# Three decay buffers and four state buffers in the scan loop of a decoder layer

## The chip, the cores and the metric

The kernel runs on one core of one Trainium2 chip. The metric is the device time of one execution in microseconds (us). A profile is one more execution of the same program, and all durations below come from it.

The engines are called as in the profile: PE (TensorE, matrix products and transposes into PSUM; PEld is its weight load), DVE (VectorE), ACT (ScalarE), POOL (GpSimd) and SP (SyncE, which here issues every DMA). Each engine runs its own instructions strictly in order and waits on semaphores that the others raise.

## The reference, cut to what matters

Eight sequences of 512 tokens with 256 channels go through one layer: a Mamba block, a slot attention with a GRU (three rounds), and a feed-forward block with a spiking output, each with a layer norm behind it. The part that the change touches is the selective scan of the Mamba block:

```
dt = softplus(dt_in @ W_dt.T + dt_bias)          # 512 tokens x 512 channels
dA  = exp(dt[..., None] * A)                     # "decay", 16 states for each channel
dBu = dt[..., None] * Bm[:, :, None, :] * u[..., None]
def step(h, e):
    da, dbu, c = e
    h = da * h + dbu                             # recurrence over the 512 tokens
    y = jnp.einsum('bdn,bn->bd', h, c)
    return h, y
```

Everything is float32.

## The kernel before, in words

The core works through the sequences one after the other, and the three blocks are software-pipelined: the body for step i runs the Mamba block of sequence i, the slot attention of sequence i-1, the first part of the feed-forward block of sequence i-2 and its spiking output (one step later, so of i-3). Steps 0 to 2 fill the pipeline (step 0 has the Mamba block alone, step 1 adds the attention, step 2 the feed-forward block), steps 3 to 7 hold all of it, and steps 8 to 10 have no Mamba block. At the end of each step all engines meet (`meet`).

The channels lie in 4 chunks of 128 (c), and the 16 states of a chunk in 8 pairs, so there are 32 groups g in a step, g = 8c + q. A group is one tile of 128 partitions x 1024 (two states x 512 tokens). The body walks through 35 slots, and each engine runs its part of slot g and then the "filler" of that slot: pieces of the other two blocks, which a table called `plan` places by hand at slot numbers. Per group the engines do this:

- ACT, line 875, `decay(g)`: two exponentials of 128x511 into the decay buffer `d_a[g % 2]`. In slot g it makes the decay of group g + 1 and then runs its filler. Its wait is `scan_done >= g - 1` for decay(g), which in slot g means that the scans 0 to g - 1 are done.
- DVE, line 1069, `mul(g)`: B x dt x u into PSUM (pb banks 1 and 2). It waits for the B rows (`bb`, three buffers, DMA) and for scan g - 1.
- DVE, line 1078, `scan(g)`: the recurrence, reads `d_a` and pb, writes `h[g % HR]`. It waits for the decay (`da_ready`), and from g = HR on for `hsum_done >= g - HR + 1`: PE must have read the buffer.
- POOL, line 443: h x C in place, raises `hc_done`.
- PE, line 645, `hsum(g)`, placed LAG = 2 slots later: eight transposes of 128x128 that add the states in PSUM bank py, raises `hsum_done`.

In slot g DVE runs scan(g), mul(g + 1) and then its filler. Behind each chunk ACT copies py to `yv` (line 888), PE transposes it back into pc (`y_back`, line 655), DVE adds u x D (line 1095, "ypost") and POOL multiplies by the gate (line 447). The feed-forward products of slot 10 and later (line 623 "up", line 631 "down") wait for ypost, because they share bank pc.

Fillers that the prediction's steps touch, with their slots:

- `gate_x` of the attention rounds 0, 1, 2 in slots 2/4, 13/15, 24/26: PE line 554, then tanh on ACT line 778 (a table load in front of it), and on ACT also lines 782 to 786 (`reset`, `keep`). `sp_ln` in slot 2 (ACT line 808) makes the softplus of the chunks 1 to 3, and POOL line 425 (`dt`) adds it up in slots 3, 6, 6.
- `keep` on POOL (line 405) in slots 4, 15, 26; `hold` on DVE (line 994) and `cand_x` on PE (line 564) in slots 6, 17, 28; `cand` in slots 7, 18, 29: tanh on ACT (line 812), then POOL lines 409 and 412, which finish the new slots state hT (`h_done`).
- `sq` and `norm` (ACT line 764, PE lines 527 and 528, ACT 769 and 771) start the next round behind `h_done`, in slots 9 and 20; `score` on DVE (line 975) in slots 10 and 21, `soft` (line 981) one slot later, `colsum`, `recol`, `spread`, `renorm` (PE 534, DVE 984 and 986, PE 539, DVE 989) in the two or three slots behind it.
- `out_stats` in slot 4 (DVE lines 916 to 921, then POOL line 393) and `out_norm` in slot 8 (DVE line 927, four tensor_scalars of 128x256 on tile reg_m), in steps 3 to 7 only.
- Weight merging on PE and ACT in slot 10 of step 0 only.

`reg_a` is one SBUF region for several uses: the first 2060 columns are the padded input `upad` of the convolution before the scan, and the decay buffers lie on the same columns. `xp` is a copy of the projected dt, B and C rows; it is read by the dt projection and by the DMAs to DRAM before the first group.

Of the kernel before, what the change touches and what calls it, by code (L numbers as in the profile page):

```python
# [26 lines left out]
ACT = mybir.ActivationFunctionType  # L27
AX = mybir.AxisListType

P = 128  # L30
BATCH, L, E = 8, 512, 256
DIN, NS, DTR, KC = 512, 16, 16, 4
# [6 lines left out]
GROUPS = DT * PAIRS  # L39
# [1 line left out]
SCALE = float(E) ** -0.5  # L41
LN_EPS, RMS_EPS = 1e-5, 1e-6
BETA, THRESHOLD, STEPS = 0.9, 1.0, 5
HR = 3
HB = 3
Q = 32

# [48 lines left out]
def decoder_layer(nc, bc_dram, x, ctx_in, cols_d, w_inT, w_xT, w_dtT, w_outT, wq_d, wk_d, wv_d, wihT, whhT, w_fcT, w_prT, out):  # L96
    with ExitStack() as ctx:
        def sb(name, shape, dt=F32):
            return ctx.enter_context(nc.sbuf_tensor(name, shape, dt))

        def ps(name, shape):
            return ctx.enter_context(nc.psum_tensor(name, shape, F32))
# [12 lines left out]
        neg_a = sb("neg_a", [P, DT * NS])  # L115
# [6 lines left out]
        rms_eps = sb("rms_eps", [P, 1])  # L122


        reg_a = sb("reg_a", [P, 2060 + HR * 1024])
        reg_y = sb("reg_y", [P, DT, L])
        upad = reg_a[:, 0:2060].rearrange("p (c t) -> p c t", c=DT)
        d_a = reg_a[:, 0:2048].rearrange("p (s n t) -> p s n t", s=2, n=2)
        h = reg_a[:, 2060:].rearrange("p (s n t) -> p s n t", s=HR, n=2)
        h2 = reg_a[:, 2060:].rearrange("p (s t) -> p s t", s=HR)  # L130
        d_a2 = reg_a[:, 0:2048].rearrange("p (s t) -> p s t", s=2)
        xn = reg_y[:, 0:2, :].rearrange("p a (b e) -> p (a b) e", e=E)
        xnT = reg_y[:, 2:4, :]
        sp = reg_y
# [5 lines left out]
        dt = sb("dt", [P, DT, L])  # L140
        dtu = sb("dtu", [P, DT, L])
        cb = sb("cb", [P, NS, L])
        xp = sb("xp", [P, L])
        bb = sb("bb", [P, HB, 2, L])
        x1 = sb("x1", [P, TT, E])
        hT = sb("hT", [P, ET, L])
# [25 lines left out]
        pb = ps("pb", [P, 4, L])  # L172
# [11 lines left out]
        s = {n: ctx.enter_context(nc.semaphore(n)) for n in COUNTS}  # L184
# [12 lines left out]
        def col(name, j):  # L197
            return cols[:, COLS[name].start + j:COLS[name].start + j + 1]
# [46 lines left out]
        def chunk_end(g):  # L245

            c, r = divmod(g - LAG, PAIRS)
            return c - 1 if 1 <= c <= DT and r == 0 else None
# [61 lines left out]
        def take(position, slot_step, mamba, slots, ffn, spikes):  # L310

            for step in plan.get(position, ()):
                kind = step[0]
                if (spikes if kind in SPIKE_STEPS else ffn if kind in FFN_STEPS else mamba if kind in MAMBA_STEPS else slots):
                    if kind in ("up", "down"):
                        slot_step(*step, back=chunks_back(position) if mamba else 0, spikes=spikes, mamba=mamba)
                    else:
                        slot_step(*step, spikes=spikes, ffn=ffn, mamba=mamba)
# [63 lines left out]
        def _(pool):  # L382
# [44 lines left out]
            def body(i, mamba, slots, ffn, spikes):  # L427
# [10 lines left out]
                for g in range(SLOTS):  # L438
                    if mamba and g < GROUPS:
                        q = g % PAIRS  # L440
                        pool.wait_ge(s["scan_done"], g + 1)
                        pool.wait_ge(s[f"cb_in{q}"], 16)
                        pool.tensor_tensor(h[:, g % HR], h[:, g % HR], cb[:, 2 * q:2 * q + 2], ALU.mult).then_inc(s["hc_done"], 1)  # L443
                    if mamba and chunk_end(g) is not None:
# [14 lines left out]
        def _(pe):  # L459
# [175 lines left out]
            def hsum(g):  # L635
# [6 lines left out]
                for j in range(2):  # L642
                    for i2 in range(TT):
                        cols_ = slice(i2 * P, (i2 + 1) * P)
                        mm = pe.matmul(py[:, cols_], h[:, g % HR, j, cols_], ident[:], is_transpose=True,  # L645
                                       start=(q == 0 and j == 0 and i2 == 0), stop=(q == PAIRS - 1 and j == 1), skip_group_check=True)
# [66 lines left out]
        def _(act):  # L713
# [105 lines left out]
            def body(i, mamba, slots, ffn, spikes):  # L819
                def filler(position):  # L820
                    take(position, slot_step, mamba, slots, ffn, spikes)

                filler("start")
                def u_tanh(j):
                    act.wait_ge(s["conv_step"], 6 * (j // 2) + 5 + j % 2)
                    act.activation(dtu[:, j], u2[:, j], ACT.Tanh, scale=0.5).then_inc(s["uth_ready"], 1)

                def z_tanh(j):
                    act.wait_ge(s["z_full"], j + 1)
                    act.activation(sz[:, j], z_banks[j], ACT.Tanh, scale=0.5).then_inc(s["zth_ready"], 1)  # L830

                def softplus_parts(c):
                    act.wait_ge(s["pre_full"], 2 + c)
                    act.activation(dt[:, c], pb[:, c, :], ACT.Relu, bias=col("dt_bias", c))
                    act.activation(sp[:, c], pb[:, c, :], ACT.Abs, bias=col("dt_bias", c)).then_inc(s["sp_abs"], 1)  # L835

                if mamba:
                    z_tanh(0)
                    z_tanh(1)
                    z_tanh(2)  # L840
                    u_tanh(0)
                    u_tanh(1)
                    z_tanh(3)
                filler("z")
                if mamba:
                    u_tanh(2)
                    u_tanh(3)
                filler("u")
                if mamba or slots:
                    act.preload_act_table_set(LN_EXP)  # L850
                if mamba:
                    act.wait_ge(s["pre_full"], 1)
                    act.activation(xp[:], pb[:, 2, :], ACT.Copy).then_inc(s["bc_kept"], 1)
                filler("x")
                if mamba:

                    softplus_parts(0)
                    act.wait_ge(s["sp_abs"], 1)
                    act.activation(sp[:, 0], sp[:, 0], ACT.Exp, scale=-1.0).then_inc(s["sp_exp"], 1)
                    act.wait_ge(s["sp_exp"], 1)  # L860
                    act.activation(sp[:, 0], sp[:, 0], ACT.Ln, bias=1.0).then_inc(s["sp_ln"], 1)  # L861
                    for c in range(1, DT):
                        softplus_parts(c)
                filler("dt")

                def decay(g):
                    c, n = g // PAIRS, 2 * (g % PAIRS)
                    if g == 0:
                        act.wait_ge(s["da_zero"], 1)
                    if g % PAIRS == 0:  # L870
                        act.wait_ge(s["dt_ready"], c + 1)
                    if g >= 2:
                        act.wait_ge(s["scan_done"], g - 1)
                    for j in range(2):
                        ins = act.activation(d_a[:, g % 2, j, 1:], dt[:, c, 1:], ACT.Exp, scale=neg_a[:, c * NS + n + j:c * NS + n + j + 1])  # L875
                    ins.then_inc(s["da_ready"], 1)

                for g in range(SLOTS):
                    if mamba:
                        if g == 0:  # L880
                            decay(0)
                        if g + 1 < GROUPS:
                            decay(g + 1)
                        if g > LAG and (g - LAG) % PAIRS == PAIRS - 1:
                            c = (g - LAG) // PAIRS
                            act.wait_ge(s["hsum_done"], PAIRS * (c + 1))
                            act.wait_ge(s["dt_ready"], DT)
                            act.activation(yv[:, c], py[:], ACT.Copy).then_inc(s["yt_ready"], 1)
                        if g == MERGE_SLOT and not slots:
                            merge_weights()  # L890
                    filler(g)
                filler("end")
                if mamba:
                    next_copies()
                    act.wait_ge(s["upad_zero"], 1)
                    u_copies(0)
                    u_copies(1)
                    if slots:
                        act.wait_ge(s["x_full"], 4 + XR * NI + 1)
                    for e in range(ET):  # L900
                        act.wait_ge(s["post_full"], e + 1)
                        act.activation(hT[:, e], px[:, e, :], ACT.Copy).then_inc(s["hT_loaded"], 1)
                    u_copies(2)
                    u_copies(3)
                meet(act, i + 2)

            iterations(act, body)


        @block.vector  # L910
        def _(dve):
# [114 lines left out]
            def body(i, mamba, slots, ffn, spikes):  # L1026
# [45 lines left out]
                def scan(g):  # L1072

                    dve.wait_ge(s["da_ready"], g + 1)
                    dve.wait_ge(s["mul_done"], g + 1)
                    if g >= HR:
                        dve.wait_ge(s["hsum_done"], g - HR + 1)
                    dve.tensor_tensor_scan(h2[:, g % HR], d_a2[:, g % 2], pb[:, 1:3, :].rearrange("p a t -> p (a t)"), 0.0,  # L1078
                                           ALU.mult, ALU.add).then_inc(s["scan_done"], 1)

                for g in range(SLOTS):
                    if mamba:
# [9 lines left out]
                        if chunk_end(g) is not None:  # L1092
                            c = chunk_end(g)
# [59 lines left out]
```

## Time and profile before

| | |
|---|---|
| median of 3 runs | 1865.69 us (1863.43 to 1866.33) |
| the profiled execution, its own time | 1863.23 us |
| its span, first to last instruction | 1861.2 us |
| busy: PE, DVE, ACT, POOL | 1366.2, 1350.9, 987.5, 898.0 us |
| DVE line 1078 (scan), 256 times | 584.6 us, 2283 ns each |
| DVE line 1069 (mul), 256 times | 314.6 us, 1229 ns each |
| POOL line 443, 256 times | 611.7 us, 2391 ns each |
| ACT line 875, 512 times | 335.6 us |
| mean granted clock of PE | 0.849 |

Busy time is a sum over the whole span. No engine is busy all the time: the shares of the two fullest are 73%. So the waits between them, read in order of time, say more than the sums.

### The profile page before, as it was taken

The page shows a single profiled execution, that of the slowest core. Times are in us where ns is not written, and L with a number is a line of the kernel's source. Part 1 is how long each engine was busy: PE and PEld are TensorE (multiplying, and loading weights), DVE is VectorE, ACT ScalarE, POOL GpSimd, SP SyncE. Part 2 cuts the span into 40 slices and gives each one's busy share as a digit, 9 for nine tenths or more (in the row PEclk, how much of TensorE's full clock was granted, in tenths as well). Part 3 has the DMA queues.
Part 4 walks back from the last instruction along what each step waited for, and adds up shares of the span by engine and source line. Part 5 has one row for each costly group of instructions (what it writes and reads, how often), then busy time and mean ns, then how long its engine had stood idle before and what let it go on. Part 6 is the DMA issues. An engine that isn't in the chain of part 4 may idle for free.

```text
span 1861.2 us, 16320 instructions
## 1 busy us (share of the span) xinstructions
PE 1366.2 (73%) x5472; PEld 826.3 (44%) x5472; DVE 1350.9 (73%) x1509; ACT 987.5 (53%) x1519; POOL 898.0 (48%) x459
## 2 busy tenths in 40 slices
PE   5555767686797758885778667887588857786975
PEld 2344344453455335552456334553355434562433
DVE  3987588957876888867888687867878778773142
ACT  4432665547663655647554655637465566534532
POOL 0665077615764266624666165642667155651110
PEclk9555978897899879998799978998799978998988
DMA  5632343205330532206321343305332153310000
GB/s 182 241 124 79 100 163 118 86 26 214 113 109 27 189 108 102 80 24 204 113 101 56 120 136 114 106 23 183 102 112 79 36 193 112 112 34 0 12 0 23
DMA packets 64762, 188.89 MB, mean 101 GB/s; under 512 B 6224, under 2 KB 22480, under 8 KB 64720
## 3 DMA queue, kind: packets, MB, share of 16 engines
q1 hardware_dynamic: 64720, 188.37, 29.3%
q8 instruction: 22, 0.36, 0.1%
q14 instruction: 20, 0.16, 0.0%
HBM read 183.62 MB, written 4.72 MB: 101 GB/s over the span
## 4 chain that ended last, share of the span: by engine, by line
PE 40%; DVE 31%; ACT 15%; issue 6%; POOL 5%; DMA 2%; ACTq 0%; DVEq 0%; POOLq 0%; SPq 0%; another core or an unknown queue 0%
DVE reg_a L1078 16%; DVE pb L1069 8%; PE py L645 6%; PE pc L631 5%; PE pc L623 4%; PE pb L486 4%; PE pb L605 3%; POOL reg_a L443 3%; ACT reg_a L875 2%; PE px L549 2%; PE px L527 2%; DMA x_out<-reg_m 2%; PE pb L587 2%; ACT xs L778 2%; DVE reg_m L927 1%
## 5 line engine op out<-in xcount | busy, mean ns | idle before, releaser
L443 POOL TENSOR_TENSOR reg_a<-reg_a,cb 128x1024 f32<-128x1024 f32 x256 | 611.7, 2391 | 438.1 <-DVE reg_a L1078 437.8
L1078 DVE TENSOR_TENSOR_SCAN reg_a<-reg_a,pb 128x1024 f32<-128x1024 f32 x256 | 584.6, 2283 | 143.5 <-ACT reg_a L875 110.2
L875 ACT ACTIVATE reg_a<-dt,neg_a 128x511 f32<-128x511 f32 x512 | 335.6, 711 | 165.3 <-DVE reg_a L1078 164.6
L645 PE MATMUL py<-ident,reg_a 128*128 128x128 f32 x2048 | 329.9, 318 | 70.6 <-POOL reg_a L443 70.6
L645 PEld LDWEIGHTS py<-ident,reg_a 128*128 128x128 f32 x2048 | 288.9, 167 | 167.6 <-POOL reg_a L443 104.9
L1069 DVE TENSOR_TENSOR pb<-bb,pb 128x1024 f32<-128x1024 f32 x256 | 314.6, 1229 | 29.7 <-ACT reg_y L835 2.6
L564 PE MATMUL pb<-ex,vw 64*128 64x512 f32 x48 | 46.9, 1075 | 146.9 <-DVE px L994 146.9
L623 PE MATMUL pc<-x2T,w_fc 128*128 128x512 f32 x224 | 119.0, 658 | 28.1 <-DVE reg_y L1095 21.2
L549 PE MATMUL px<-hT,whh 128*128 128x512 f32 x288 | 137.4, 613 | 0.4 <-ACT xs L778 0.4
L631 PE MATMUL pc<-w_pr,reg_m 128*128 128x256 f32 x448 | 109.8, 396 | 7.0 <-ACT y_sb L798 4.1
L405 POOL TENSOR_TENSOR xs<-xs,hT 128x1024 f32<-128x1024 f32 x24 | 56.6, 2358 | 96.2 <-ACT xs L786 96.2
L527 PE MATMUL px<-hT,gT 128*64 128x512 f32 x96 | 61.1, 772 | 56.8 <-ACT xs L764 56.8
L631 PEld LDWEIGHTS pc<-w_pr,reg_m 128*128 128x128 f32 x448 | 86.1, 200 | 24.6 <-ACT y_sb L798 6.5
L793 ACT ACTIVATE reg_m<-pc 128x512 f32<-128x512 f32 x56 | 33.3, 595 | 115.1 <-PE pc L623 103.0
L425 POOL TENSOR_TENSOR dt<-dt,reg_y 128x512 f32<-128x512 f32 x32 | 40.7, 1283 | 102.7 <-ACT reg_y L861 95.8
L549 PEld LDWEIGHTS px<-hT,whh 128*128 128x128 f32 x288 | 55.2, 200 | 70.6 <-issue 66.2
L778 ACT ACTIVATE xs<-px,half_b 128x512 f32<-128x512 f32 x72 | 46.7, 681 | 63.8 <-PE pb L554 46.3
L564 PEld LDWEIGHTS pb<-ex,vw 64*128 64x128 f32 x48 | 11.3, 293 | 154.4 <-DVE px L994 154.4
L549 PE MATMUL pb<-hT,whh 128*128 128x512 f32 x96 | 56.4, 719 | 31.8 <-ACT reg_y L835 31.8
L486 PE MATMUL pb<-reg_y,w_in 128*128 128x512 f32 x144 | 67.3, 612 | 11.1 <-ACT reg_y L728 11.1
L1042 DVE SCALAR_TENSOR_TENSOR u<-reg_a,cols,u 128x512 f32<-128x512 f32 x96 | 64.2, 740 | 11.2 <-SPq L332 11.2
L623 PEld LDWEIGHTS pc<-x2T,w_fc 128*128 128x128 f32 x224 | 41.8, 207 | 64.2 <-issue 35.1
(174 smaller groups left out, 2259.5 us busy)
## 6 DMA issues: line engine op xcount, KB each, us to landing
bb<-bc_rows SPq DMA_DIRECT2D x256, 512.0 KB, 3.7
cb<-bc_rows SPq DMA_DIRECT2D x64, 512.0 KB, 6.0
xin<-x_in SPq DMA_DIRECT2D x9, 512.0 KB, 3.6
xs<-x_in SPq DMA_DIRECT2D x8, 512.0 KB, 3.6
x_out<-reg_m SPq DMA_DIRECT2D x8, 512.0 KB, 3.4
w_in<-w_inT_in SPq DMA_DIRECT2D x1, 1024.0 KB, 7.1
w_fc<-w_fcT_in SPq DMA_DIRECT2D x1, 1024.0 KB, 10.9
w_pr<-w_prT_in SPq DMA_DIRECT2D x1, 1024.0 KB, 13.1
```

Source lines behind the costliest of these rows:

```text
L443: pool.tensor_tensor(h[:, g % HR], h[:, g % HR], cb[:, 2 * q:2 * q + 2], ALU.mult).then_inc(s["hc_done"], 1)
L486: mm = pe.matmul(pb[:, c, :], w_in[:, e, c * P:(c + 1) * P], xnT[:, e], start=(e == 0), stop=(e == ET - 1))
L527: pe.matmul(px[0:M, 0, :], gT[:, e], hT[:, e], start=(e == 0), stop=(e == ET - 1))
L549: pe.matmul(gate_bank[j], whh[:, e, j * P:(j + 1) * P], hT[:, e], start=(e == 0), stop=False)
L623: mm = pe.matmul(unit_bank(half, "up", j, mamba), w_fc[:, e, f * P:(f + 1) * P], x2T[:, e], start=(e == 0), stop=(e == ET - 1))
L631: mm = pe.matmul(bank[:, (i2 % 2) * E:(i2 % 2 + 1) * E], hid[:, j, i2 * P:(i2 + 1) * P], w_pr[:, half * UPS + j], start=(j == 0), stop=(j ...
L645: mm = pe.matmul(py[:, cols_], h[:, g % HR, j, cols_], ident[:], is_transpose=True, start=(q == 0 and j == 0 and i2 == 0), stop=(q == PAIR ...
L778: act.activation(xs[:, j // 2, (j % 2) * L:(j % 2 + 1) * L], gate_bank[j], ACT.Tanh, scale=0.5, bias=half_b[:, j:j + 1]).then_inc(s["trz_r ...
L875: ins = act.activation(d_a[:, g % 2, j, 1:], dt[:, c, 1:], ACT.Exp, scale=neg_a[:, c * NS + n + j:c * NS + n + j + 1])
L1042: dve.scalar_tensor_tensor(u2[:, c], upad[:, c, t:t + L], col("conv_w", c * KC + t), u2[:, c], ALU.mult, ALU.add).then_inc(s["conv_step"], 1)
L1069: dve.tensor_tensor(pb[:, 1:3, :], bb[:, g % HB], pb[:, 0:1, :].to_broadcast([P, 2, L]), ALU.mult).then_inc(s["mul_done"], 1)
L1078: dve.tensor_tensor_scan(h2[:, g % HR], d_a2[:, g % 2], pb[:, 1:3, :].rearrange("p a t -> p (a t)"), 0.0, ALU.mult, ALU.add).then_inc(s["s ...
```

## The change

`d_a` gets three buffers in place of two and `h` four in place of three. ACT makes decay(0), decay(1) and decay(2) in slot 0, and from there decay(g + 2) in slot g. The constants in the waits follow the number of buffers. The decay buffers now have columns of their own length (3072) ahead of `h`, and `xp` lies in the last buffer of `h`.

```diff
-HR = 3
+HR = 4
+DR = 3
...
-        reg_a = sb("reg_a", [P, 2060 + HR * 1024])
+        reg_a = sb("reg_a", [P, (DR + HR) * 1024])
...
-        d_a = reg_a[:, 0:2048].rearrange("p (s n t) -> p s n t", s=2, n=2)
-        h = reg_a[:, 2060:].rearrange("p (s n t) -> p s n t", s=HR, n=2)
+        d_a = reg_a[:, 0:DR * 1024].rearrange("p (s n t) -> p s n t", s=DR, n=2)
+        h = reg_a[:, DR * 1024:].rearrange("p (s n t) -> p s n t", s=HR, n=2)
+        xp = h2[:, HR - 1, 0:L]
...
-        xp = sb("xp", [P, L])
...
-                    act.activation(xp[:], pb[:, 2, :], ACT.Copy).then_inc(s["bc_kept"], 1)
+                    act.activation(xp, pb[:, 2, :], ACT.Copy).then_inc(s["bc_kept"], 1)
...
-                    if g >= 2:
-                        act.wait_ge(s["scan_done"], g - 1)
+                    if g >= DR:
+                        act.wait_ge(s["scan_done"], g - DR + 1)
                     for j in range(2):
-                        ins = act.activation(d_a[:, g % 2, j, 1:], dt[:, c, 1:], ACT.Exp, scale=...)
+                        ins = act.activation(d_a[:, g % DR, j, 1:], dt[:, c, 1:], ACT.Exp, scale=...)
                     ins.then_inc(s["da_ready"], 1)
...
                         if g == 0:
                             decay(0)
-                        if g + 1 < GROUPS:
-                            decay(g + 1)
+                        if g == 0:
+                            decay(1)
+                        if g + 2 < GROUPS:
+                            decay(g + 2)
...
-                    dve.tensor_tensor_scan(h2[:, g % HR], d_a2[:, g % 2], ...)
+                    dve.tensor_tensor_scan(h2[:, g % HR], d_a2[:, g % DR], ...)
```

## Rows read from the trace of the kernel before

**Rows 1.** The page: busy time of each engine; last chain's shares of the span.

```profile
PE 1366.2 (73%) x5472; PEld 826.3 (44%) x5472; DVE 1350.9 (73%) x1509; ACT 987.5 (53%) x1519; POOL 898.0 (48%) x459
...
PE 40%; DVE 31%; ACT 15%; issue 6%; POOL 5%; DMA 2%; ACTq 0%; DVEq 0%; POOLq 0%; SPq 0%; another core or an unknown queue 0%
```

**Rows 2.** Waits, whole span: engine and line, waited for, total us, times, longest.

```profile
DVE reg_a L1078 <- ACT reg_a L875: 110.2, 51, 5.9
DVE reg_a L1078 <- PE py L645: 26.4, 26, 2.1
```

**Rows 3.** Waits of DVE in the groups of step 4, 847 to 1012 us.

```profile
DVE reg_a L1078 <- ACT reg_a L875: 15.3, 7, 5.7
DVE reg_a L1078 <- PE py L645: 4.4, 4, 1.9
DVE sc L975 <- ACT rt L771: 3.0, 1, 3.0
```

**Rows 4.** The chain that ended last: the same piece of two steps.

```profile
800.16 5.18 PE pb L605 x24
...
1015.24 5.18 PE pb L605 x24
```

**Rows 5.** Timeline of ACT, step 4: start, duration, then the idle time before.

```profile
854.39 1.33 ACT L875 ACTIVATE reg_a<-dt,neg_a 128x511 f32<-128x511 f32 x2 [1.02 <-DVE reg_a L1078]
...
861.35 0.69 ACT L778 ACTIVATE xs<-px,half_b 128x512 f32<-128x512 f32 x1 [4.33 <-PE pb L554]
...
868.00 2.56 ACT L875 ACTIVATE reg_a<-dt,neg_a 128x511 f32<-128x511 f32 x4
...
872.70 1.04 ACT L786 ACTIVATE xs<-xs 128x1024 f32<-128x1024 f32 x1
```

**Rows 6.** Timeline of DVE, step 4, slots 4 to 8.

```profile
869.36 2.29 DVE L1078 TENSOR_TENSOR_SCAN reg_a<-reg_a,pb 128x1024 f32<-128x1024 f32 x1 [5.70 <-ACT reg_a L875]
...
874.74 1.69 DVE L921 TENSOR_SCALAR out_var<-out_mv 128x4 f32<-128x4 f32 x1
...
892.71 5.17 DVE L927 TENSOR_SCALAR reg_m<-reg_m,out_mv,out_rstd 128x256 f32<-128x256 f32 x4
...
1016.61 1.39 DVE L927 TENSOR_SCALAR x<-x,x_mv,x_rstd 128x256 f32<-128x256 f32 x4 [1.13 <-POOL x_rstd L393]
```

**Rows 7.** Timeline of POOL, step 4, slots 4 to 8.

```profile
874.05 2.35 POOL L405 TENSOR_TENSOR xs<-xs,hT 128x1024 f32<-128x1024 f32 x1
876.51 1.02 POOL L393 TENSOR_TENSOR out_rstd<-out_var,mhalf 128x4 f32<-128x4 f32 x1
...
884.72 2.49 POOL L425 TENSOR_TENSOR dt<-dt,reg_y 128x512 f32<-128x512 f32 x2
...
892.38 2.35 POOL L412 TENSOR_TENSOR hT<-xs 128x1024 f32<-128x1024 f32 x1
894.68 2.40 POOL L443 TENSOR_TENSOR reg_a<-reg_a,cb 128x1024 f32<-128x1024 f32 x1
```

**Rows 8.** Timeline of DVE, step 4, two later stalls.

```profile
929.70 2.29 DVE L1078 TENSOR_TENSOR_SCAN reg_a<-reg_a,pb 128x1024 f32<-128x1024 f32 x1 [3.07 <-ACT reg_a L875]
...
982.94 2.29 DVE L1078 TENSOR_TENSOR_SCAN reg_a<-reg_a,pb 128x1024 f32<-128x1024 f32 x1 [2.29 <-ACT reg_a L875]
```

**Rows 9.** Timeline of DVE, step 0 (first two rows) and step 1.

```profile
48.34 2.29 DVE L1078 TENSOR_TENSOR_SCAN reg_a<-reg_a,pb 128x1024 f32<-128x1024 f32 x1 [1.04 <-ACT reg_a L875]
...
98.54 2.29 DVE L1078 TENSOR_TENSOR_SCAN reg_a<-reg_a,pb 128x1024 f32<-128x1024 f32 x1 [3.27 <-ACT reg_a L875]
...
229.57 2.29 DVE L1078 TENSOR_TENSOR_SCAN reg_a<-reg_a,pb 128x1024 f32<-128x1024 f32 x1 [2.81 <-ACT reg_a L875]
250.75 2.29 DVE L1078 TENSOR_TENSOR_SCAN reg_a<-reg_a,pb 128x1024 f32<-128x1024 f32 x1 [5.86 <-ACT reg_a L875]
```

**Rows 10.** Busy us by stretch (PE, PEld, DVE, ACT, POOL), then PE's granted clock.

```profile
876.00:886.00 10.00, 0.97 (x2) 0.51 (x4) 9.70 (x8) 2.67 (x4) 7.37 (x6) 0.53 0.28 100
...
848.00:1012.00 164.00, 121.74 (x522) 75.88 (x522) 133.98 (x117) 93.05 (x137) 106.64 (x49) 0.85 0.34 118
```

More of the change, by code:

```diff
@@ L122, in decoder_layer @@
         rms_eps = sb("rms_eps", [P, 1])
-        reg_a = sb("reg_a", [P, 2060 + HR * 1024])
+        reg_a = sb("reg_a", [P, (DR + HR) * 1024])
         reg_y = sb("reg_y", [P, DT, L])
         upad = reg_a[:, 0:2060].rearrange("p (c t) -> p c t", c=DT)
-        d_a = reg_a[:, 0:2048].rearrange("p (s n t) -> p s n t", s=2, n=2)
-        h = reg_a[:, 2060:].rearrange("p (s n t) -> p s n t", s=HR, n=2)
-        h2 = reg_a[:, 2060:].rearrange("p (s t) -> p s t", s=HR)
-        d_a2 = reg_a[:, 0:2048].rearrange("p (s t) -> p s t", s=2)
+        d_a = reg_a[:, 0:DR * 1024].rearrange("p (s n t) -> p s n t", s=DR, n=2)
+        h = reg_a[:, DR * 1024:].rearrange("p (s n t) -> p s n t", s=HR, n=2)
+        h2 = reg_a[:, DR * 1024:].rearrange("p (s t) -> p s t", s=HR)
+        d_a2 = reg_a[:, 0:DR * 1024].rearrange("p (s t) -> p s t", s=DR)
+        xp = h2[:, HR - 1, 0:L]
         xn = reg_y[:, 0:2, :].rearrange("p a (b e) -> p (a b) e", e=E)
@@ L871, in decay @@
                         act.wait_ge(s["dt_ready"], c + 1)
-                    if g >= 2:
-                        act.wait_ge(s["scan_done"], g - 1)
+                    if g >= DR:
+                        act.wait_ge(s["scan_done"], g - DR + 1)
                     for j in range(2):
-                        ins = act.activation(d_a[:, g % 2, j, 1:], dt[:, c, 1:], ACT.Exp, scale=neg_a[:, c * NS + n + j:c * NS + n + j + 1])
+                        ins = act.activation(d_a[:, g % DR, j, 1:], dt[:, c, 1:], ACT.Exp, scale=neg_a[:, c * NS + n + j:c * NS + n + j + 1])
                     ins.then_inc(s["da_ready"], 1)
@@ L1077, in scan @@
                         dve.wait_ge(s["hsum_done"], g - HR + 1)
-                    dve.tensor_tensor_scan(h2[:, g % HR], d_a2[:, g % 2], pb[:, 1:3, :].rearrange("p a t -> p (a t)"), 0.0,
+                    dve.tensor_tensor_scan(h2[:, g % HR], d_a2[:, g % DR], pb[:, 1:3, :].rearrange("p a t -> p (a t)"), 0.0,
                                            ALU.mult, ALU.add).then_inc(s["scan_done"], 1)
```

## The prediction, as it was put on record

> **What bounds the kernel now.** I began with the page. Neither of the fullest engines, PE and DVE, is busy for more than 73% of the span [rows 1], so the waits decide. In the waits, the scan of DVE stands twice: 110.2 us in 51 waits on the decay of ACT, and 26.4 us in 26 waits on `hsum` of PE. Both are in [rows 2]. The change aims at the first two sums: 136.6 us together, 7% of the time, and that is the ceiling.
>
> Next, the repetition. The same piece of the chain comes back after 1015.2 - 800.2 = 215.0 us [rows 4], so the five full steps 3 to 7 are copies of one another and one of them can be read for all. In the groups of step 4 DVE is busy 134.0 of 164 us [rows 10], and waits 15.3 us on the decay in 7 waits and 4.4 us on `hsum` in 4 [rows 3]. Not all of the 15.3 can go: the first scan of a step waits 2.8 us because decay(0) comes only after the softplus [rows 9], and decay(0) is not made earlier. That leaves 12.5 + 4.4 = 16.9 us in a full step.
>
> Why the decay is late is seen on ACT. Its next decay is made at 854.39, in slot 2, then come tanh at 861.35 (after 4.3 us of waiting for PE), the softplus, table loads, and only at 868.00 the following decay [rows 5]. DVE's scan(4) waits 5.7 us for that [rows 6]. ACT is not too slow here; it stands behind a filler.
>
> **The change, part by part.**
>
> *Decay two groups ahead.* decay(g + 2) in slot g waits for `scan_done >= g`, which is what decay(g + 1) waited for in slot g before. So ACT does the same work at the same moments, each time for a group later, and nothing that is queued behind on ACT is put off. One decay more (1.3 us) stands in slot 0, where ACT until now waited for scan(0), and none in slot 30. The number of exponentials, 512, and of table loads stays. No DMA is added or moved, on no queue. Cost: 0. The bound from below is 0 as well, from above the 1.3 us once a step if the wait in slot 0 didn't cover it, 8 x 1.3 = 10 us.
>
> *Fourth h buffer.* scan(g) waits for hsum(g - 4) and not for hsum(g - 3), a whole group of 3.5 us (2.29 + 1.23) more room against waits of at most 2.1 us [rows 2]. They all go.
>
> *xp in the last h buffer, the longer region, six in place of four columns to clear:* all readers of xp are done before the first scan, scan(3) writes there more than 10 us later, the clearing is a POOL instruction in a stretch where it idles. Cost 0.
>
> Now what DVE meets once the stalls are gone, walked through step 4 with the durations of its rows, each engine in its order:
>
> (a) decay(4) is now the one made at 854.39, so scan(4) starts at 869.36 - 5.70 = 863.7: 5.7 us. Behind it `out_var`, an operation on 4 columns, took 1.69 us, until POOL's line 405 was over [rows 6, 7]; at its new time, 869.1, POOL ends line 443 of group 4 within 0.3 us. The gain is 6.7 us at scan(5), and decay(5), made at 868.0 as ever, is just in time.
>
> (b) It does not last. POOL's queue in these slots hangs on ACT's line 786, which ends at 873.7 as before [rows 5], because the gates wait for PE and not for the scans. From there POOL has line 405 (2.35), the rstd (1.0), lines 443 of groups 5 and 6 (4.7), two dt (2.5), line 443 of group 7 (2.4), lines 409 and 412 (4.7), and line 443 of group 8 (2.4), 20.1 us without a gap, to 893.8; before it ended at 897.1 [rows 7]. POOL so gains 3.3 us and no more. DVE reaches `out_norm` at 892.7 - 6.7 = 886.0. These four tensor_scalars took 5.17 us where their twins on another tile took 1.39 [rows 6]: the first of them ended when POOL's line 412 ended, the next when line 443 did, and then POOL was idle. In the new order POOL is never idle there, so each of the four waits for one POOL operation, to about 894. DVE's gain falls from 6.7 to 3.5 us. The Trainium skill says why, in "SBUF — State Buffer", section "SBUF: two separate sides": GpSimd and a VectorE operation in a two-port mode lock the shared ports for a whole instruction, and the other one blocks fully. This trace agrees (5.17 against 1.39 us). By that rule, as by the row, DVE can't pass here before POOL lets it.
>
> (c) `h_done` of round 0 comes 3.2 us earlier, so do `norm`, `y_back`, ypost, and the first `up` behind it, and ACT's exponentials for `soft`: still 3.5 us. Then the 1.9 us wait of scan(12) on `hsum` is gone (5.4), some 0.6 us is lost at `recol`, which comes before PE's `colsum` (4.8), and scan(15) no longer waits 3.07 us [rows 8] (7.8). Two `hsum` waits in slots 19 and 21, 1.9 of the 2.5 us left in 4.4, go (9.7).
>
> (d) At `score` of round 2 DVE waits 3.0 us for ACT [rows 3]. That hangs on `h_done` and on ACT's copies of the down products, which I find 8.1 us earlier, not 9.7: the wait becomes 4.6 us and the gain 8.1. Two short decay waits behind it, 1.2 us, bring it to 9.3, the 2.29 us wait at 982.94 [rows 8] to 11.6; ypost of the third chunk, which now waits for PE's `y_back`, takes 1.4 back, and behind the last scan PE's down products hold DVE as before. The end of the groups comes 10 us earlier.
>
> So a full step gains 10 of 16.9 us: 5 x 10 = 50 us. Of what is left after (b), 16.9 - 5.7 = 11.2 us, DVE keeps 6.5, a share of 0.58.
>
> *The filling steps.* All waits on the decay less those of five full steps are 110.2 - 76.5 = 33.7 us, on `hsum` 26.4 - 22.0 = 4.4 us. Of these 38.1 the first scans keep 1.0 + 2.8 + 2.8 [rows 9], which leaves 31.5 us. Step 0 has neither attention nor output, its 3.3 us at 98.54 (behind the merging) goes whole. In steps 1 and 2 the large wait (5.86 in step 1 [rows 9]) meets the same POOL queue at slot 4, there with no out_norm to be paid before and after; `h_done` moves by some 0.7 us only, so they give 0.7 each. The rest, 31.5 - 3.3 - 11.7 = 16.5 us, at the share of 0.58 gives 9.6. Sum: 3.3 + 1.4 + 9.6 = 14.3 us.
>
> **Sum:** 50 + 14.3 = 64.3 us, from the profiled execution's 1863.2 us to 1798.9. The median of the runs shown is 2.5 us above that execution, so the forecast is 1865.7 - 64.3 = 1801.4 us, call it 1801.
>
> **The rivals.**
>
> *A: the gain is swallowed, by POOL and by the attention's own chain.* If each later stall, like the one of (b), only turns into a wait for POOL, for `h_done` or for PE's products, what stays is 3.5 us in a full step, plus one or two more, say 5: 25 us, with 3.3 + 3 in the filling steps 31 us, 1834 us. For it: `score` already holds DVE 3.0 us [rows 3], and POOL has no gap from line 409 to the end of line 443 of group 8 in the kernel before either [rows 7]. Against it: from slot 9 on POOL has gaps, 106.6 of 164 us busy [rows 10].
>
> *B: more than I count.* PE's granted clock is 0.85 in these groups [rows 10], between its levels of 1.2 GHz (0.5) and 2.4 GHz (1.0); it is 0.53 in the stretch where PE, busy 1.0 of 10 us, waits for `hold` [rows 10], and that wait gets shorter. If it held full speed there, the products on the chain between 886 and 915 would be some 4 us shorter, 5 x 4 = 20 us: 1781. Nothing of it is in my sum, since those waits stay. The Trainium skill, "TensorE: Matmul & The Clock Gate", section "HAM oscillation — how this bites in real kernels", has gaps between bursts as what throws TensorE back; no row here shows what shorter gaps give.
>
> *C: slower, by the clock.* With DVE ahead, PE's short work comes in smaller pieces between waits. PE's busy time in the groups is 121.7 us at 0.85 [rows 10]; I take 40% of the 164 us, 66 us, as PE's part of the path (an estimate, by its share of the last chain [rows 1]). At a granted clock x it grows by 66 x (0.85/x - 1). At 0.75 that is 9 us a step and eats the gain; below 0.74 it decides, and at 0.70 it is 14 us: 4 us slower a full step, 20 in all, less the 3 of step 0: about 1883. Against it: the work of PE is the same and its waits get shorter.
>
> *D: no change.* Were ACT's filler to hold the decay by two groups wherever it does so now, the second buffer would move the wait and not remove it. The stretch from 854.39 to 868.00 is 13.6 us [rows 5], longer than two groups (7 us); but without the wait DVE has scan(4), mul(5) and `out_stats` to do from 863.7 on, some 5.5 us, and the later waits are under 3.1 us. Time: 1865.
>
> **How the numbers follow.** My forecast, a gain of 45 to 80 us: 0.60. A: 0.23. B: 0.08. C: 0.04. D: 0.05. The range that leaves out no more than two in ten reaches into B and most of A: 1782 to 1836. A difference of 0.2% is about what a measurement of this kernel can tell from none. Faster: 0.60 + 0.23 + 0.08 = 0.91. Same 0.05, slower 0.04.
>
> **What would show it.** In the waits, scan on decay falls from 110.2 to about 21 us (the eight first scans) and scan on `hsum` to nearly 0. The step is 205 us. The group of line 927 on reg_m goes from 5.2 to about 8 us for four, in slot 8. `score` in round 2 waits about 4.6 us for ACT. I am wrong if `out_norm` costs as before (then the gain is larger), if scan waits for the decay in slot 3 too, if POOL's line 443 gets few gaps behind slot 9, or if the granted clock in the groups leaves 0.85 by more than 0.03.

## The result, and the profile after

| | before | after |
|---|---|---|
| median of 4 runs | 1864.74 us (1863.43 to 1866.33) | 1799.61 us (1799.23 to 1799.80) |
| span of the profiled execution | 1861.2 us | 1797.8 us |
| ratio of the runs | | 0.965, 95% interval 0.9633 to 0.9667 |
| one full step | 215.0 us [rows 4] | 204.9 us |
| granted clock of PE, mean | 0.849 | 0.858 |

The kernel became 65 us faster; a gain of 64 us, to 1801 us, was forecast. The forecast was right in its direction and its size. Below it is seen that most of its steps hold too, that one thing it left at nothing, PE's clock, moved with the change, and that what it took from rows alone can be shown by experiments.

The waits of DVE, whole span, in the changed kernel (line numbers there are a few higher: the scan is line 1081, the decay 876, hsum 646, line 443 of POOL is 444, and 927 is 930):

```profile
DVE sc L978 <- ACT rt L772: 55.8, 12, 13.4
DVE y_sb L966 <- PE pc L632: 55.2, 14, 26.9
...
DVE reg_a L1081 <- ACT reg_a L876: 24.8, 10, 2.8
...
DVE reg_y L1098 <- PE pc L656: 17.0, 10, 6.3
...
DVE rc L987 <- PE px L535: 10.7, 9, 3.0
```

The scan waits 24.8 us for the decay where it waited 110.2, and its 26.4 us for `hsum` are gone from the list [rows 2]. The longest of the ten is 2.8 us, the first scan of a step. What became longer stands around it: ypost (line 1098) now waits for PE's `y_back` (17.0 us, 7.3 before), `recol` (line 987) for `colsum` (10.7, 5.5 before), `score` (line 978) for 55.8 us (53.3) and line 966, behind PE's down products, for 55.2 us (50.6).

The same step as in [rows 3], its groups at 825 to 979 us, and the start of the same piece of the chain as in [rows 4]:

```profile
DVE y_sb L966 <- PE pc L632: 3.8, 2, 2.2
DVE sc L978 <- ACT rt L772: 3.2, 1, 3.2
DVE reg_a L1081 <- ACT reg_a L876: 2.8, 1, 2.8
DVE sums L984 <- ACT ex L776: 2.5, 1, 2.5
DVE rc L987 <- PE px L535: 0.9, 1, 0.9
```

```profile
777.57 5.18 PE pb L606 x24
982.47 5.18 PE pb L606 x24
```

16.9 us of waits on decay and `hsum` went from this step, and the step is 10.1 us shorter. So 7 us came back. DVE's timeline of slots 4 to 8 shows where, beside [rows 6]:

```profile
841.35 2.29 DVE L1081 TENSOR_TENSOR_SCAN reg_a<-reg_a,pb 128x1024 f32<-128x1024 f32 x1
...
846.73 0.22 DVE L924 TENSOR_SCALAR out_var<-out_mv 128x4 f32<-128x4 f32 x1
...
857.72 2.21 DVE L1060 TENSOR_TENSOR pb<-dt,u 128x512 f32<-128x512 f32 x1
...
864.86 7.27 DVE L930 TENSOR_SCALAR reg_m<-reg_m,out_mv,out_rstd 128x256 f32<-128x256 f32 x4
```

Scan(4) no longer waits (5.70 before). `out_var` takes 0.22 us and not 1.69. But `out_norm`, the last row, takes 7.27 us for four operations where it took 5.17, and line 1060, the product dt x u, takes 2.21 us; before, at the same place, it took this:

```profile
887.08 0.68 DVE L1057 TENSOR_TENSOR pb<-dt,u 128x512 f32<-128x512 f32 x1
```

Neither stands as a wait in any view: both are engine time that looks like work. POOL's timeline beside them, as [rows 7]:

```profile
851.41 2.36 POOL L406 TENSOR_TENSOR xs<-xs,hT 128x1024 f32<-128x1024 f32 x1 [4.49 <-ACT xs L787]
...
859.33 2.94 POOL L426 TENSOR_TENSOR dt<-dt,reg_y 128x512 f32<-128x512 f32 x2
862.24 2.34 POOL L444 TENSOR_TENSOR reg_a<-reg_a,cb 128x1024 f32<-128x1024 f32 x1
864.54 2.35 POOL L410 TENSOR_TENSOR xs<-xs,dtu 128x1024 f32<-128x1024 f32 x1
866.97 2.34 POOL L413 TENSOR_TENSOR hT<-xs 128x1024 f32<-128x1024 f32 x1
869.27 2.40 POOL L444 TENSOR_TENSOR reg_a<-reg_a,cb 128x1024 f32<-128x1024 f32 x1
```

POOL stands idle 4.49 us for ACT's line 787, and from there has no gap until 871.67. DVE's `out_norm` ends at 872.1. Its first three operations took 2.18, 2.49 and 2.44 us, each until one of POOL's last three was over (866.9, 869.3, 871.7), and the fourth was short.

### The profile page after: what moved, and what is told of

It is laid out like the page before. It is cut to its first block, busy times and chain, and to the rows that moved or that the text cites. A ratio compares the mean times of both kernels' runs of the same rounds, so it can differ in the third digit from the quotient of the medians.

```text
span 1797.8 us, 16320 instructions
## 1 busy us (share of the span) xinstructions
PE 1359.0 (76%) x5472; PEld 818.6 (46%) x5472; DVE 1370.9 (76%) x1509; ACT 984.8 (55%) x1519; POOL 896.8 (50%) x459
## 4 chain that ended last, share of the span: by engine, by line
DVE 36%; PE 35%; ACT 11%; issue 7%; POOL 7%; DMA 2%; DVEq 0%; ACTq 0%; POOLq 0%; SPq 0%; another core or an unknown queue 0%
DVE reg_a L1081 19%; DVE pb L1072 9%; PE pc L632 5%; POOL reg_a L444 4%; PE pb L487 4%; PE py L646 4%; PE pb L606 3%; PE pc L624 3%; PE px L550 3%; PE px L528 2%; DVE reg_m L930 2%; DMA x_out<-reg_m 2%; PE pb L588 2%; DVE u L1045 1%; ACT reg_a L876 1%
## 5 line engine op out<-in xcount | busy, mean ns | idle before, releaser
L1081 DVE TENSOR_TENSOR_SCAN reg_a<-reg_a,pb 128x1024 f32<-128x1024 f32 x256 | 584.6, 2284 | 34.9 <-ACT reg_a L876 24.8
L876 ACT ACTIVATE reg_a<-dt,neg_a 128x511 f32<-128x511 f32 x512 | 331.8, 710 | 102.0 <-DVE reg_a L1081 101.2
L646 PEld LDWEIGHTS py<-ident,reg_a 128*128 128x128 f32 x2048 | 280.2, 163 | 183.2 <-POOL reg_a L444 120.2
L565 PE MATMUL pb<-ex,vw 64*128 64x512 f32 x48 | 41.7, 964 | 85.1 <-DVE px L997 85.1
L528 PE MATMUL px<-hT,gT 128*64 128x512 f32 x96 | 61.3, 773 | 55.8 <-ACT xs L765 55.8
L794 ACT ACTIVATE reg_m<-pc 128x512 f32<-128x512 f32 x56 | 33.4, 596 | 106.8 <-PE pc L624 94.7
L550 PEld LDWEIGHTS px<-hT,whh 128*128 128x128 f32 x288 | 55.2, 200 | 70.7 <-issue 66.4
L891 ACT ACTIVATE reg_y<-py 128x512 f32<-128x512 f32 x32 | 18.7, 586 | 115.5 <-PE py L646 115.5
L550 PE MATMUL pb<-hT,whh 128*128 128x512 f32 x96 | 55.8, 711 | 31.8 <-ACT reg_y L836 31.8
L487 PE MATMUL pb<-reg_y,w_in 128*128 128x512 f32 x144 | 68.2, 619 | 10.7 <-ACT reg_y L729 10.7
```

What stands on the lines that cost most here:

```text
L487: mm = pe.matmul(pb[:, c, :], w_in[:, e, c * P:(c + 1) * P], xnT[:, e], start=(e == 0), stop=(e == ET - 1))
L528: pe.matmul(px[0:M, 0, :], gT[:, e], hT[:, e], start=(e == 0), stop=(e == ET - 1))
L550: pe.matmul(gate_bank[j], whh[:, e, j * P:(j + 1) * P], hT[:, e], start=(e == 0), stop=False)
L876: ins = act.activation(d_a[:, g % DR, j, 1:], dt[:, c, 1:], ACT.Exp, scale=neg_a[:, c * NS + n + j:c * NS + n + j + 1])
L1081: dve.tensor_tensor_scan(h2[:, g % HR], d_a2[:, g % DR], pb[:, 1:3, :].rearrange("p a t -> p (a t)"), 0.0, ALU.mult, ALU.add).then_inc(s[" ...
```

## The experiments

The kernel before ran beside each group of them, at 1864.4 to 1864.9 us. Times are medians; ratios are to the kernel before, with their 95% intervals. "The changed kernel" has 1799.6 us.

**1. Decay ahead, three h buffers.**

```diff
-HR = 4
+HR = 3
 DR = 3
```

> The changed kernel with three h buffers in place of four. Theory (the decay order carries the gain, hsum waits are mostly refilled by other waits): 1803 us, 1800 to 1812; the scan's waits on hsum come back with 10 to 30 us in all, and score of round 2 waits less than 3.2 us. Rival (both halves are needed, each alone only moves the wait): above 1830 us.

Measured: 1820.4 us (1814.8 to 1820.8), ratio 0.9752 (0.9734 to 0.9771). The direction was as the theory had it, the size was not, and 1820 lies outside the range I gave: without the fourth h buffer the kernel is 20.7 us slower, and not 3. So the decay ahead alone brings 44 of the 65 us. The waits on `hsum` come back with 26.1 us, as expected. The time has another part besides, seen in the chain of its full steps:

```profile
580.81 5.18 PE pb L606 x24
786.59 5.18 PE pb L606 x24
997.32 5.18 PE pb L606 x24
1203.15 5.18 PE pb L606 x24
1413.75 5.18 PE pb L606 x24
1619.55 5.18 PE pb L606 x24
```

Identical steps take 205.8 and 210.7 us in turn. Laid side by side, step for step, they part mainly at two places, both on PE. At one of them, `cand_x` in slot 17, PE has waited the same 3.09 us in both:

```profile
716.62 0.69 PE L565 MATMUL pb<-ex,vw 64*128 64x512 f32 x1 [3.09 <-DVE px L997]
...
924.65 1.22 PE L565 MATMUL pb<-ex,vw 64*128 64x512 f32 x1 [3.09 <-DVE px L997]
```

The same product takes 0.69 us in one step and 1.22 in the next; in the second it comes 2.3 us later from the step's start. With the products behind it this costs 1.9 us. The other place is the first products after the engines have met (line 600), 2.0 us. A further 0.9 us goes at the last down products of the step (line 632, 2.75 us in place of 1.89). Between the profiled executions lie 21.0 us. Two such steps carry 11.7 of them (210.7 against 204.8 in the changed kernel), the three others 3.0 (205.8), and the filling steps 8.0 (the first row above is 572.79 in the changed kernel), 3.0 of these in step 0, where the scan behind the weight merging waits 2.97 us for `hsum`; the end is 1.7 us shorter.

**2. Four h buffers alone.**

```diff
-DR = 3
+DR = 2
...
-                            decay(1)
-                        if g + 2 < GROUPS:
-                            decay(g + 2)
+                        if g + 1 < GROUPS:
+                            decay(g + 1)
```

(`h` stays where it is, so that `upad` keeps its columns.)

> Four h buffers, but two decay buffers and the decay one group ahead as before. Theory: the 26 us of waits on hsum go, half of it is lost again at the decay waits and at score: 1852 us, 1845 to 1862. Rival (both halves needed): within 3 us of 1865. Rival (h carries the gain): under 1830 us.

Measured: 1864.8 us, ratio 0.9999 (0.999 to 1.0009). There is no change: my 1852 was wrong, and the first rival ("both halves needed") is borne out for this half. DVE's waits in this kernel:

```profile
DVE reg_a L1079 <- ACT reg_a L876: 119.7, 57, 5.9
DVE sc L976 <- ACT rt L772: 65.5, 12, 13.4
```

No wait on `hsum` is left. The 26.4 us were passed on: 9.5 to the decay (110.2 before) and 12.2 to `score` (53.3 before), each a few slots later, and the rest to the end of a step. A full step is 215.1 us.

**3. The buffers without the order.**

```diff
-                        if g == 0:
-                            decay(1)
-                        if g + 2 < GROUPS:
-                            decay(g + 2)
+                        if g + 1 < GROUPS:
+                            decay(g + 1)
...
                 elif step == "sp_exp":
+                    act.wait_ge(s["sp_abs"], DT)
```

The added wait puts down an order that ACT had kept by its other waits.

> The changed kernel's buffers (three and four) with the order of before: decay(g + 1) in slot g. Theory (ACT is late because it stands behind its filler, so the order is what pays and a buffer alone nothing): as h_only within 4 us, about 1850 us, and the 5.7 us wait of scan(4) stays. Rival (the wait for the buffer is what held ACT): about 1800 us.

Measured: 1863.6 us, ratio 0.9996 (0.9986 to 1.0005): as h_only within 1.2 us. My absolute figure was off for the same reason as in 2. The wait that the theory named stands:

```profile
656.42 2.29 DVE L1080 TENSOR_TENSOR_SCAN reg_a<-reg_a,pb 128x1024 f32<-128x1024 f32 x1 [5.70 <-ACT reg_a L877]
```

So the decay was not late for want of a buffer. It was late because it stood behind a filler in ACT's order. The third buffer by itself pays nothing, it only allows the order.

**4. Three ahead.** Four decay buffers, three h buffers (for four of both SBUF has no room).

```diff
-HR = 4
-DR = 3
+HR = 3
+DR = 4
...
                             decay(1)
-                        if g + 2 < GROUPS:
-                            decay(g + 2)
+                            decay(2)
+                        if g + 3 < GROUPS:
+                            decay(g + 3)
```

> Four decay buffers, decay three groups ahead, three h buffers (there is no room for four of both): to be compared with decay_only. Theory (two groups cover every filler; what is left are the first scans): within 2 us of decay_only, waits of the scan on the decay about 21 to 25 us in both. Rival (a longer lead goes on paying): at least 10 us faster than decay_only.

Measured: 1815.7 us (1815.2 to 1820.4), ratio 0.9745 (0.9728 to 0.9762), to be compared with decay_only at 0.9752 (0.9734 to 0.9771). The medians are 4.7 us apart, but both kernels have runs near 1815 and near 1820, and the intervals overlap: no difference that these runs can tell. The scan waits 29.5 us for the decay, 34.1 in decay_only. A third group of lead covers little that two don't, and these runs show no 10 us.

**5. `out_norm` without the shared port.** The four tensor_scalars of out_norm in steps 3 to 7 read PSUM in place of reg_m: the kernel leaves out the norm of the output for these steps.

```diff
+                for i2 in range(TT):
+                    dve.tensor_scalar(accv[:, i2], pb[:, 0, 0:E], mv[:, i2, 0:1], rstd[:, i2:i2 + 1], ALU.subtract,
...
-                    norm_apply("out", memv, accv)
+                    if mamba:
+                        out_norm()
+                    else:
+                        norm_apply("out", memv, accv)
```

> The changed kernel, but the four tensor_scalars of out_norm in steps 3 to 7 read a PSUM bank in place of the tile reg_m, so what they write is not the output's norm. Theory (they wait because VectorE and GpSimd share an SBUF port, and this holds DVE some 5.4 us a step; PE's y_back, ready 4.2 us before ypost in the changed kernel, then becomes the next to hold): the four take 1.7 us and not 7.1, a step is 3.5 to 4 us shorter, 1781 us, 1777 to 1790. Rival (it only waits there for what it would wait for a slot later, h_done and y_back): within 4 us of 1800.

Measured: 1765.7 us, ratio 0.9465 (0.9449 to 0.9481), 33.9 us faster than the changed kernel and below the range I gave (1777 to 1790). A group of its lines:

```profile
L930 DVE TENSOR_SCALAR reg_m<-pb,out_mv,out_rstd 128x256 f32<-128x256 f32 x20 | 9.5, 536 | 0.0
```

They take 536 ns each; with the input in PSUM, only the result and the two scalars in SBUF, and POOL as busy as ever, they no longer wait. In a full step DVE is 5.5 us earlier behind them, then 4.3 us at ypost, where PE's `y_back` now holds it (1.16 us), and then 6.7 us. The last jump goes with PE's clock. First the changed kernel, then this one:

```profile
880.08 3.78 PE L624 MATMUL pc<-x2T,w_fc 128*128 128x512 f32 x4 [4.11 <-DVE reg_y L1098]
883.66 2.57 PE L550 MATMUL px<-hT,whh 128*128 128x512 f32 x4
```

```profile
869.41 1.99 PE L624 MATMUL pc<-x2T,w_fc 128*128 128x512 f32 x4
871.23 1.88 PE L550 MATMUL px<-hT,whh 128*128 128x512 f32 x4
```

Where PE waited 4.11 us for ypost, the first `up` takes 3.78 us; where it did not wait, 1.99. The granted clock is 0.58 from 880 to 886 us in the changed kernel and 1.00 from 869.4 to 873 us in this one. DVE's `soft` hangs on these products.

**6. The clock by itself.** PE gets useless work where it waited, in steps 2 to 7: four matmuls of 128x512 whose result is overwritten unread.

```diff
             def ffn_up(half, j, back, mamba):
+                if mamba and half == 0 and j == 0:
+                    for _ in range(4):
+                        pe.matmul(px[:, 1, :], whh[:, 0, 0:P], hT[:, 0], start=True, stop=True)
```

> The changed kernel, with four matmuls of 128x512 more on PE, whose result is overwritten unread, in slot 10 of steps 2 to 7, where PE waits 4.1 us for ypost before the first up product. Theory (that product takes 3.8 us and the next gates 2.6 us because PE stood idle and its clock was halved, and DVE's soft waits for them): they take 1.9 us each, soft comes 2.5 us earlier a step, 12 us faster than the changed kernel in all, 1787 us, 1783 to 1794. Rival (the length of these products has another cause): the added work changes nothing or makes it slower, 1800 to 1810 us.

Measured: 1791.3 us, ratio 0.9611 (0.9594 to 0.9627): 8.3 us faster with more work.

```profile
873.29 3.60 PE L623 MATMUL px<-hT,whh 128*128 128x512 f32 x8
877.71 1.99 PE L627 MATMUL pc<-x2T,w_fc 128*128 128x512 f32 x4 [0.82 <-DVE reg_y L1101]
879.53 1.88 PE L550 MATMUL px<-hT,whh 128*128 128x512 f32 x4
```

Both products came out at 1.99 and 1.88 us as expected, at a granted clock of 1.00 (877.7 to 881.3 us). PE is 2.6 us ahead behind them, and the step is 3.2 us shorter; the rest is won at its last down products. That the whole is 8 and not 12 us or more lies in the other steps: the full ones take 201.7, 201.7, 204.2, 201.8 and 204.3 us. In the first of the slow ones the first two groups of products at line 600 took 2.55 and 3.03 us, behind a wait of 2.32 us; in the step before it they took 1.96 and 1.88 us, behind a wait of 2.35 us.

**7. POOL's `keep` one slot later.** Only line 406 on POOL moves, to the slots 5, 16, 27, behind line 444 of that group.

```diff
+        for k, position in enumerate((5, 16, 27)):
+            place(position, ("keep_pool", k))
...
-                elif step == "keep":
+                elif step == "keep_pool":
                     pool.wait_ge(s["z_ready"], 2 * k + 1)
```

> The changed kernel, with POOL's line 406 (keep) one slot later in each round, behind line 444 of that group. Theory (POOL stands idle up to 4.5 us in slot 4 for ACT's line 787 and its queue of the slots 5 to 8 is late by that, which holds out_norm and h_done): h_done of round 0 comes 3 us earlier, a step is 3 to 4 us shorter, 1776 us, 1765 to 1788. Rival (POOL is not on the path, the attention's chain is): within 4 us of 1800.

Measured: 1779.2 us, ratio 0.9544 (0.9528 to 0.9559), 20.4 us faster than the changed kernel. A full step is 201.3 us. DVE is 2.9 us earlier behind `out_norm` and 3.5 us at `soft`. So POOL's idle 4.5 us in slot 4 and the queue behind it were on the path, as step (b) has it.

**8. decay(0) before the softplus of chunk 3** and before ACT's filler at "dt", which holds two exponentials of `score`.

```diff
-                    for c in range(1, DT):
-                        softplus_parts(c)
-                filler("dt")
+                    softplus_parts(1)
+                    softplus_parts(2)
...
+                if mamba:
+                    decay(0)
+                    softplus_parts(3)
+                filler("dt")
...
-                        if g == 0:
-                            decay(0)
                         if g == 0:
                             decay(1)
```

The wait of experiment 3 in `sp_exp` is in here too, and in 9 and 11.

> The changed kernel, with decay(0) on ACT ahead of the softplus parts of chunk 3 and of the two exponentials of score. Theory (the 2.8 us in which the first scan of steps 1 to 7 waits for decay(0) lie on the path and two decays ahead don't touch them): the wait goes, 2.4 us a step, 1783 us, 1778 to 1790. Rival (score and the gates come later by as much and hold DVE in slots 0 to 3): within 4 us of 1800.

Measured: 1780.3 us (1777.3 to 1785.8), ratio 0.9552 (0.953 to 0.9574), 19.3 us faster. The scan's waits on the decay fall to 6.0 us in all. In a full step 2.9 us are won at the first scan, 0.2 of them lost again at the second and 0.95 at `out_var`, which meets POOL (1.16 us in place of 0.22), and most of that is won back up to `recol`. The full steps take 201.3 to 204.3 us, again not all alike.

**9. Both, 7 and 8.**

> keep_late and decay0_early in one kernel, with the whole computation. Theory (two waits at two places on DVE's path): most of the two gains adds up, 1760 us, 1750 to 1772. Rival (both meet the same next wait, at out_norm or at score): no more than the better of the two alone.

Measured: 1771.9 us, ratio 0.9505 (0.9489 to 0.952), 7 us better than the better one alone and 12 worse than the theory: of 39.6 us that the two won apart, 27.7 stay. Against experiment 7 DVE is 2.55 us ahead at the first scan of a step; 0.8 us of it are gone at `out_var` (1.04 us in place of 0.22), 1.1 at `soft` and `recol`, whose products on PE are slower than in 7, and the rest at PE, where `cand_x` in slot 17 is slow again (1.06 us a product in place of 0.59). DVE ends level at `score` of round 2. A full step is 201.4 us, the same as in 7; all that is gained lies in the filling steps. In the full steps the rival is right; in the whole the time lies at the upper end of the range I gave.

**10. `out_norm` on ACT.** The whole computation stands, in ACT's slot 8; `out_nb` is -mean x rstd, made by one small multiply more on DVE and one on POOL.

```diff
+                elif step == "out_norm":
+                    act.wait_ge(s["out_nb"], 1)
+                    for i2 in range(TT):
+                        act.activation(acc[:, i2 * E:(i2 + 1) * E], mem[:, i2 * E:(i2 + 1) * E], ACT.Identity,
+                                       scale=stats["out"][3][:, i2:i2 + 1], bias=out_nb[:, i2:i2 + 1]).then_inc(s["out_norm"], 1)
```

> The changed kernel, with out_norm done by ACT in slot 8 (scale by rstd, bias -mean x rstd; one small multiply more on DVE and on POOL), so the whole computation stands. Theory (it is DVE's wait for the shared port that costs, not the work): nearly as norm_from_psum measured, 1765.7 us, less 1.7 us of DVE work a step and with 1 us more on POOL: 1764 us, 1755 to 1775. Rival (ACT in slot 8 delays sq and norm of round 1 by as much): 1790 us or more.

Measured: 1766.2 us, ratio 0.9475 (0.9459 to 0.9491), 33.4 us faster than the changed kernel and 2 us from the 1764 expected.

```profile
L809 ACT ACTIVATE reg_m<-reg_m,out_nb,out_rstd 128x256 f32<-128x256 f32 x32 | 16.6, 591 | 29.2 <-POOL out_nb L423 29.1
```

ACT does the same four tiles in 2.07 us of a full step (849.85 us) beside a busy POOL, at a place where it had been idle: its wait behind them is 1.70 us where it was 3.39.

**11. 7, 8 and 10 together.**

> norm_on_act together with keep_late and decay0_early. Theory (keep_late was worth most where it let out_norm through, so it adds little now; decay0_early still takes 2.8 us at the head of each step, less what the clock and score take back): 1752 us, 1740 to 1765. Rival (all meet at the same waits for PE): no faster than norm_on_act.

Measured: 1740.1 us (1739.1 to 1742.1), ratio 0.9336 (0.932 to 0.9352): 59.5 us faster than the changed kernel and 124 faster than the one before, with the whole computation. A full step is 194.5 us; the mean granted clock of the span is 0.874. The estimate of 1752 was 12 us too high, and the time lies just at the lower end of the range.

## Why the prediction was right

Times of the changed kernel are shifted by 848.35 - 825.94 = 22.4 us, from first scan to first scan of step 4, so that they stand beside those of the rows.

*Costs put at 0* (ACT's order, xp, the longer region): nothing in the trace speaks against them. The number of instructions is the same, 16320, and the exponentials of ACT from 854.39 to slot 4 begin at the same moments.

*(a)* scan(4) at 863.8 (863.7 forecast), `out_var` at 0.22 us, a gain at scan(5) of 7.0 us (6.7). Right.

*(b)* The step on which the sum hangs. POOL's queue ends at 894.1 (893.8), `out_norm` holds DVE until 894.5 ("about 894"), the gain falls from 7.0 to 3.3 us (3.5). Right, and experiments 5, 7 and 10 show it as a cause: take the port away, or let POOL be earlier, and the time comes back. One piece of it I missed: DVE reached `out_norm` at 887.3 and not 886.0, since line 1060, with two operands in SBUF, had waited for POOL as well (2.21 us). So three of the four operations waited for POOL, and not all four. It cost next to nothing, because `out_norm` would have waited there. What the Trainium skill says ("SBUF — State Buffer", section "SBUF: two separate sides") covers both kinds: a VectorE operation in a two-port mode, or one with two SBUF inputs against a GpSimd operation that reads SBUF. The 7.27 and 2.21 us here agree with it, and so do the 536 ns with the input in PSUM.

*(c)* 3.3 at `soft` (3.5), 5.3 at scan(12) (5.4), 4.6 behind `recol` (4.8), 7.6 at scan(15) (7.8), 9.4 at scan(21) (9.7). Right within 0.3 us each.

*(d)* The term that was mis-sized. `score` of round 2 waits 3.2 us and not 4.6, and the gain there is 9.3 us and not 8.1. The chain ahead of it, `cand_x`, `y_back`, the down products, was 1.1 us faster than I had taken from the rows. For PE had waited 6.38 us before `cand_x` in the kernel before, and 2.17 us after the change, and the same product takes 1.22 us before and 0.69 us after:

```profile
942.70 1.22 PE L564 MATMUL pb<-ex,vw 64*128 64x512 f32 x1 [6.38 <-DVE px L994]
...
936.00:953.00 17.00, 9.93 (x43) 7.43 (x42) 15.55 (x12) 6.28 (x11) 13.80 (x7) 0.80 0.33 116
```

```profile
912.74 0.69 PE L565 MATMUL pb<-ex,vw 64*128 64x512 f32 x1 [2.17 <-DVE px L997]
...
912.00:929.00 17.00, 13.31 (x71) 9.77 (x72) 15.21 (x11) 7.79 (x12) 16.92 (x9) 1.00 0.36 127
```

The granted clock (third number from the end) is 0.80 before and 1.00 after. The two stretches don't begin at the same work; from 904 to 921 us, where the wait itself lies, it is 1.00 after the change too. From `cand_x` to the down products PE wins 1.8 us by it. Later DVE is 12.7 us ahead at scan(26) (11.6), ypost takes 0.7 us back and not 1.4, and `next_var`, 4 columns at 958.10, meets POOL and takes 1.65 us (0.17 before), which I had not seen coming. The misses about cancel: the step came out 10.1 us shorter, 10 forecast. So the total of a step was right partly by luck.

*The filling steps.* Over steps 3 to 7 the kernel won 51.3 us (50), before them 12.3 (14.3), behind them nothing: 63.4 us between the two profiled executions, 64.3 forecast. The share of 0.58 that I carried over was good enough for the sum. From first scan to first scan, step 0 won 2.9 us (3.3), step 1 won 3.1 and step 2 won 7.1; the first scan of step 0 came 0.8 us later (49.15 us after 48.34; from 48.7 to 49.5 in experiments 1, 3 to 7 and 10). Whether the new layout costs that, the one trace of the kernel before can't tell.

*The signs I named.* The scan waits 24.8 us for the decay (about 21) and not at all for `hsum`, the step is 204.9 us (205), `out_norm` takes 7.27 us (about 8), and the granted clock in the groups is 0.86 (0.85 before). Only `score` missed.

*The rivals.* A (the gain swallowed) is right as a mechanism, at its one place; elsewhere the stalls did pass through. B (the clock gives more) is right in kind. At the place that I named, between 886 and 915, nothing changed in the products behind ypost: the first `up` takes 3.78 us before and after; it moved in slot 17 instead. Experiment 6 shows what the clock was worth at the place that I had named: 3.2 us in a step where nothing else changes. C has its truth in experiment 1, where two full steps of five lose 4.9 us each against the others, 4.8 of them at products of PE that take longer. D is refuted: scan(4) no longer waits.

*What I had not put as a rival* is that the two halves don't add. The fourth h buffer alone is worth 0, with the decay ahead 20.7 us, and some 10 of these (2 x 4.9) go with the clock. I took 26.4 us of waits to go and a share to stay, and never asked what each half does alone.

Open: why the clock falls at 3.09 us of waiting in one step and not in the next. The runs show only that the two steps differ by 0.3 us in time at the first such place (line 600) and by 2.3 us at the second. The length of the wait doesn't decide it: at line 600 of experiment 1 the first product group took 1.95 us behind a wait of 2.06, 2.93 behind 2.35, and 1.96 behind 2.49. Not tried, for want of room in SBUF: three groups of lead with four h buffers.

## What to carry to other kernels

When a producer stands in order behind other work, give it a lead in its own queue and the buffers that the lead needs; a buffer without the order measured as nothing here (experiments 2 and 3), and the order without the next stage's buffer as two thirds of the gain (experiment 1). Walk the queue of every engine once past the stall that goes, up to the first engine that did not move (here POOL, tied to an event that stayed where it was): that walk, done over one step, came within 0.3 us for most stalls; what it could not tell was PE's clock. And look for waits that are booked as work: an operation on 4 columns of 1.7 us, or the same operation at 0.35 and at 1.8 us, was a wait here, and moving it to an engine without the conflict was worth half as much as the whole change.

## What the runs showed of the hardware

- A VectorE tensor_scalar of 128x256 from SBUF to SBUF took 5.17 and 7.27 us for four beside a busy GpSimd, 1.39 us beside an idle one, and 536 ns each with its input in PSUM, beside a GpSimd just as busy. ScalarE did the same tile in 591 ns there.
- A tensor_tensor with both operands in SBUF and its result in PSUM, 0.68 us at the same place before, took 2.21 us when it met a GpSimd operation already running.
- PE's granted clock after a wait was not the same each time: behind 3.09 us of waiting the same product took 0.69 us in one step and 1.22 us in the next. A kernel of equal steps so ran in steps of 205.8 and 210.7 us in turn. Its runs lay up to 6 us apart; whether by the same cause no trace shows.
- Four unneeded matmuls of 128x512 in a wait of 4.1 us, in six steps, made the kernel 8.3 us faster; the granted clock of the products behind them went from 0.58 to 1.00.
